# A two-layer transformer on one core: experts work on the rows routed to them, and routing runs ahead of attention

## What is computed

```python
xn = _layernorm(x)
x = x + attn0(xn) + ffn0(xn)     # 16 heads of 8; ffn0: silu gate, hidden 384, int weights / 127
xn = _layernorm(x)
x = x + attn1(xn) + moe(xn)      # attn1: block mask of 64 x 64; moe: 8 experts, hidden 256
```

```python
probs = softmax(xf @ gate_w.T)
top_p, top_i = top_k(probs, 2)
w = top_p / (sum(top_p) + 1e-9)
capacity = int(1.25 * T / E)                 # 320
oh = one_hot(top_i, E)
rank = cumsum(oh, axis=0) - 1                # over tokens, for each choice and expert
keep = sum(rank * oh, -1) < capacity
comb = einsum('tk,tke->te', w * keep, oh)
for e in range(E):
    y = silu(xf @ gate_proj_w[e].T) * (xf @ up_proj_w[e].T) @ down_proj_w[e].T
    out = out + comb[:, e:e + 1] * y
```

## Time and profile before

| | us |
|---|---|
| median of 3 runs | 647.14 (646.85 to 649.95) |
| the profiled execution | 649.82 |
| its span | 648.1 |

### The profile page before, as it was taken

The page is one execution under the profiler, slowest core; times in us unless marked ns, Lnnn a source line. Parts: engine busy times, 40 slices in busy tenths (PEclk is TensorE's granted clock), DMA queues, the critical chain, the costliest instruction groups (busy, mean ns, idle before and its releaser), DMA issues.

```text
span 648.1 us, 10352 instructions
## 1 busy us (share of the span) xinstructions
PE 563.7 (87%) x3834; PEld 226.0 (35%) x3834; DVE 509.8 (79%) x890; ACT 340.1 (52%) x402; POOL 121.5 (19%) x209
## 2 busy tenths in 40 slices
PE   4173789799889988989999999999999999999996
PEld 2020122142124223313454435353444343445443
DVE  4497679989986987897878888979888988774443
ACT  2000576666686665665535455545455545555562
POOL 6424061232314022221112020220001000000000
PEclk9655799999999998998999999999999999999999
DMA  2698726005302541445013331025050000000000
GB/s 69 159 185 126 237 86 123 2 30 122 49 1 98 56 45 13 110 44 53 2 51 70 33 39 18 2 99 51 3 67 0 3 1 0 19 2 17 1 1 17
DMA packets 125220, 34.08 MB, mean 53 GB/s; under 512 B 103458, under 2 KB 123442, under 8 KB 124338
## 3 DMA queue, kind: packets, MB, share of 16 engines
q1 hardware_dynamic: 125170, 33.41, 28.0%
HBM read 18.05 MB, written 13.63 MB: 49 GB/s over the span
## 4 chain that ended last, share of the span: by engine, by line
PE 59%; DVE 20%; SPq 7%; issue 5%; DMA 5%; ACT 4%; POOL 1%; ACTq 0%; DVEq 0%
PE ps L535 11%; PE ps L506 11%; DVE mx L797 10%; PE ps L545 9%; PE ps L536 8%; PE ps L490 7%; PE ps L475 4%; SPq L333 3%; DVE xs L852 3%; PE ps L438 2%; DMA QO<-mT 2%; DVE th L818 2%; SPq L321 2%; PE ps L559 2%; DVE h_T L831 2%
## 5 line engine op out<-in xcount | busy, mean ns | idle before, releaser
L683 ACT ACTIVATE PT<-ps 128x1024 f32<-128x1024 f32 x256 | 260.4, 1024 | 221.1 <-PE ps L490 219.6
L797 DVE TENSOR_REDUCE mx<-ps 128x2 f32<-128x1024 f32 x256 | 307.6, 1220 | 51.0 <-PE ps L475 49.7
L506 PE MATMUL ps<-PT,Vp 128*32 128x512 f32 x1024 | 138.1, 612 | 0.4 <-ACT o_sb L689 0.4
L475 PE MATMUL ps<-KO,QO 48*128 48x512 bf16 (+1 forms) x512 | 103.6, 406 | 33.2 <-DMA KO<-z 13.6
L490 PE MATMUL ps<-QO,KO 59*128 59x512 bf16 x512 | 101.1, 391 | 18.9 <-DMA QO<-mT 14.5
L818 DVE SCALAR_TENSOR_TENSOR th<-th,ps 128x512 f32<-128x512 f32 x76 | 52.1, 686 | 48.1 <-ACT th L698 47.0
L490 PEld LDWEIGHTS ps<-QO,KO 59*128 59x128 bf16 x512 | 24.7, 93 | 167.7 <-issue 85.3
L535 PE MATMUL ps<-xnT,eg 128*128 128x512 f32 x128 | 72.0, 644 | 10.6 <-DVE mx L797 10.2
L545 PEld LDWEIGHTS ps<-ed,h_T 128*128 128x128 f32 x512 | 62.1, 192 | 16.0 <-issue 14.8
L536 PE MATMUL ps<-xnT,eu 128*128 128x512 f32 x128 | 65.6, 594 | 0.0
L545 PE MATMUL ps<-ed,h_T 128*128 128x128 f32 x512 | 62.4, 275 | 0.3 <-DVE h_T L831 0.3
(11 more groups left out here) (134 smaller groups left out, 389.8 us busy)
## 6 DMA issues: line engine op xcount, KB each, us to landing
z<-part SPq DMA_DIRECT2D x16, 384.0 KB, 2.6
z<-part SPq DMA_DIRECT2D x16, 256.0 KB, 2.9
QO<-z SPq DMA_DIRECT2D x64, 48.0 KB, 2.7
KO<-z SPq DMA_DIRECT2D x64, 48.0 KB, 2.7
QO<-z SPq DMA_DIRECT2D x6, 384.0 KB, 7.3
KO<-z SPq DMA_DIRECT2D x6, 384.0 KB, 9.2
z<-part SPq DMA_DIRECT2D x16, 128.0 KB, 2.7
QO<-mT SPq DMA_DIRECT2D x96, 4.0 KB
```

What stands on the lines that cost most here:

```text
L475: mm = pe.matmul(ps[:, 2 * pair + half, :], rows_of(QO[u % 3], half, 2 * s + jj, rows, (qt, qt + 1)), rows_of(KO[u % 3], half, 2 * s + jj, ...
L506: last = pe.matmul(ps[32 * g:32 * g + 32, PV_BANK, :], Vp[u % 3][:, k, head(s, g), :], PT[:, (2 * t + g % 2) % 4, g // 2, :], start=(s % 2 ...
L683: act.activation(PT[:, e % 4], ps[:, 2 * pair:2 * pair + 2, :], ACT.Exp).then_inc(exp_done, 1)
L797: dve.tensor_reduce(mx[:, a, qt, col:col + 5:4], ps[:, 2 * pair:2 * pair + 2, :], AX_X, ALU.max, negate=True).then_inc(max_read, 1)
```

## The change

An expert now works on places: each has 640, of which 320 are for first and 320 for second choices. A token's two copies of its normalized row go to their places in a DRAM tensor by indirect DMA, with the row's destination and weight behind it; a copy that isn't kept goes to a row of its own behind the places. All experts run in the last two units: the list `expert_work` (transposing the places, gate pairs of 320 columns, outputs of 640 rows) is laid out two items a slot from slot 4 of unit 6 and three a slot in unit 7, which it leaves at slot 8. ScalarE scales the outputs by the weights, GpSimd sends them to the tokens by indirect DMA, and at the end two tensors of results are loaded and added. Routing and the transposed normalized input are made three units ahead in place of one and two, V one ahead in place of two. The buffers of V are two rather than three, those of the transposed input four.

```diff
-            if layer(u) == 1:
-                return SLOTS_U * seq(u) + slot
-            return HB * seq(u) + slot - 9 if 9 <= slot < 9 + HB else None
-        def expert_at(u, slot):
-            if u < B or u == B and slot < 2 or slot % 2:
-                return None
-            return E * seq(u) + slot // 2 - 1
+            return HB * u + slot - 9 if u < B and 9 <= slot < 9 + HB else None
+        expert_work = [("places", 0), ("places", 1)] + [("gate1", m) for m in range(4)]
+        for e in range(E):
+            expert_work += [("places", e + 2)] * (e + 2 < E)
+            if e + 1 < E:
+                first = 4 * (e + 1)
+                expert_work += [("gate1", first), ("gate1", first + 1), ("expert", e),
+                                ("gate1", first + 2), ("gate1", first + 3)]
+            else:
+                expert_work.append(("expert", e))
+        def expert_work_at(u, slot):
+            if u == U - 2 and slot >= EXPERTS_FROM:
+                a = 2 * (slot - EXPERTS_FROM)
+                return expert_work[a:a + 2]
+            if u == U - 1:
+                a = 2 * (SLOTS_U - EXPERTS_FROM) + 3 * slot
+                return expert_work[a:a + 3]
+            return []
...
+        def empty_places(sp):
+            sp.wait_ge(empty_ready, 2)
+            dst = x_places[0:N_PLACES].rearrange("(e p j) d -> p e j d", p=P, j=JE)
+            for e in range(E):
+                sp.dma_start(dst[:, e, :, 0:D], zero_f[:, 0:D].unsqueeze(1).to_broadcast([P, JE, D])).then_inc(emptied, 16)
+                sp.dma_start(dst[:, e, :, D:ROW], empty[:, e * JE:(e + 1) * JE, :]).then_inc(emptied, 16)
+            for k in range(2):
+                sp.dma_start(y_tokens[k * T:(k + 1) * T].rearrange("(p n) d -> p n d", p=P),
+                             zero_f[:, 0:D].unsqueeze(1).to_broadcast([P, T // P, D])).then_inc(emptied, 16)
...
+        def load_results(sp, b):
+            if b == 0:
+                sp.wait_ge(y_sent[0], 16 * JE * (E // 2))
+                sp.wait_ge(y_sent[1], 16 * JE * (E // 2))
+                sp.wait_ge(pv_done, SLOTS_U * (U - 1))
+            for k in range(2):
+                src = y_tokens[k * T + b * S:k * T + (b + 1) * S].rearrange("(t p) d -> p t d", p=P)
+                sp.dma_start(results_of(b)[:, k], src).then_inc(y_in[b], 16)
...
+        def scatter(pool, p):
+            b = seq(p)
+            if b == 0:
+                pool.wait_ge(emptied, N_EMPTIED)
+            pool.wait_ge(place_ready, b + 1)
+            pool.wait_ge(xn_twice, b + 1)
+            for t in range(NT):
+                for k in range(2):
+                    pool.indirect_dma_start(out=x_places[:], out_offset=bass.IndirectOffsetOnAxis(
+                        ap=place_i[:, b, t, k:k + 1], axis=0), in_=xe[p % 2][:, t, k, :],
+                        in_offset=None).then_inc(scattered, 16)
+        def send_results(pool, e):
+            if e == 0:
+                pool.wait_ge(meta_in, 16 * E)
+            pool.wait_ge(y_copied, e + 1)
+            for j in range(JE):
+                pool.indirect_dma_start(out=y_tokens[:], out_offset=bass.IndirectOffsetOnAxis(
+                    ap=meta[:].bitcast(I32)[:, e, j, 0:1], axis=0), in_=y_sb[e % 2][:, j, :],
+                    in_offset=None).then_inc(y_sent[e % 2], 16)
...
+        def places_copy(act, e):
+            act.wait_ge(places_ps, e + 1)
+            if e >= 2:
+                act.wait_ge(up_ps[1], 4 * (e - 1))
+            act.copy(places_T[e % 2][:], across(pair_of("places", e), 0, PLACES)).then_inc(places_ready, 1)
+        def result_copy(act, e):
+            act.wait_ge(expert_ps, e + 1)
...
+            if e >= 2:
+                act.wait_ge(y_sent[e % 2], 16 * JE * (e // 2))
+            for j in range(JE):
+                last = act.activation(y_sb[e % 2][:, j, :], across(pair_of("expert", e), j * P, (j + 1) * P),
+                                      ACT.Copy, scale=meta[:, e, j, 1:2])
+            last.then_inc(y_copied, 1)
...
+            if slot == 11 and f < U:
+                pe.wait_ge(on_ready, 2 * u + 1)
+                xnT_mms(pe, f, SIDE)
+            if slot == 12 and f < U and layer(f) == 1:
+                pe.wait_ge(xnT_ready, f + 1)
+                router_mms(pe, f)
...
         def last_vector(dve):
-            add_expert(dve, E * B - 1)
             normalize_out(dve, U - 1, 1)
+            for b in range(B - 1):
+                add_results(dve, b)
             residual(dve, U - 1)
+            add_results(dve, B - 1)
```

More of the change, by code:

```diff
@@ L256, in build @@
                 if gate_at(u, slot) is not None:
-                    taken.append((f"gate{layer(u)}", gate_at(u, slot)))
-                if expert_at(u, slot) is not None:
-                    taken.append(("expert", expert_at(u, slot)))
-        taken.append(("expert", E * B - 1))
+                    taken.append(("gate0", gate_at(u, slot)))
+                taken += expert_work_at(u, slot)
         turn = {job: i for i, job in enumerate(taken)}
@@ L337, in sync_unit @@
             p, n = u + 2, u + 1
+            if u == U - 2:
+                for e in range(2):
+                    load_places(sp, e)
+                load_meta(sp)
+                for e in range(2, 4):
+                    load_places(sp, e)
             max_rows(sp, u, 1)
@@ L422, in pool_unit @@
                 parts(pool, p, 1)
+            if f < U:
+                deviation(pool, f)
+                normalize(pool, f)
             if n < U:
                 residual_base(pool, n)
+            if f < U and layer(f) == 1:
+                second_rows(pool, f)
+            if u == U - 2:
+                send_results(pool, 0)
+            if n < U:
                 split_max(pool, n, 0)
+            if p < U and layer(p) == 1:
+                scatter(pool, p)
         def xnT_mms(pe, p, bank):
@@ new lines, in expert_out, with out_mms @@
+        def expert_out(pe, e):
+            pe.wait_ge(h_ready[1], 4 * (e + 1))
+            pair = take_pair(pe, "expert", e)
+            for j in range(JE):
+                for i in range(EB):
+                    last = pe.matmul(across(pair, j * P, (j + 1) * P), h1_T[:, e % 2, i, j * P:(j + 1) * P],
+                                     ed[:, e, i, :], start=(i == 0), stop=(i == EB - 1))
+            last.then_inc(expert_ps, 1)
+        def out_mms(pe, u, tiles):
+            L = layer(u)
+            if tiles[0] == 0:
+                pe.wait_ge(onT_ready, u + 1)
+                if L == 0:
+                    pe.wait_ge(h_ready[0], HB * (u + 1))
+            for t in tiles:
@@ L1113, in _ @@
                 sync_unit(sp, u)
-            store_x(sp, U - 1)
+            for b in range(B):
+                load_results(sp, b)
+            for b in range(B):
+                store(sp, b)
             sp.wait_ge(stored, 16 * B)
@@ L1131, in _ @@
                 pool_unit(pool, u)
+            for e in range(3, E):
+                send_results(pool, e)
         @block.vector
```

432 lines of the change are left out of this document (254 added, 178 removed).

## The result

The changed kernel took 608.09 us (median of 4 runs, 607.81 to 613.51) beside 648.55 us for the kernel before in the same comparison (646.85 to 650.00, 4 runs): a ratio of 0.939, interval [0.937, 0.942]. It is faster, but 33 us above the 575 predicted, and outside the range of 557 to 602.

A forecast was written before the change was run, and what follows sets the result against it. TensorE was taken to bound units 4 to 7, with neither TensorE nor VectorE full in units 1 to 3. 648.1 + 11.4 - 72.2 - 13.6 + 1.9 = 575.6 us of span; predicted 575 us, range 557 to 602.

The forecast's parts named there:

- the one on the indirect DMAs: GpSimd, units 2 to 5 and the result sends: 1.2 us per indirect DMA, 25 us free for eight scatters, all hidden.
- The clock: Rival: units 4 and 5 fall to half clock, 84 us each, 635 us in all; chance 0.02.
- Emptying transfers at 0: 18 SyncE transfers at the end of unit 0, 12 us of issue: 0 delay to maxima rows, bounds 0 and 15 us.
- units 4 and 5: They lose all expert work: 56.6 and 51.0 us, together 107.6 against 179.8, a change of -72.2.
- the tail: After unit 7: six additions, 4.1 us, fill 3.01 idle us and two more follow; 12.0 us, +1.9.
- unit 7's first half: Slots 0 to 7 of unit 7 take three expert items each: 53 us with 3 for the rest.
- the return path: Result sends from unit 7's slot 3.5, landed by 62 us, loads done at 71, where attention ends: hidden, nothing to spare.
- Unit 6: Slots 0 to 3 have nothing added, the other 12 two expert items each: 77 us, before 86.6.
- pairs and VectorE cost more: Rival: routing work and new waits add 5 us in each of four units, 595 us; range 588 to 605, chance 0.09.
- Slower than before: Rival: scatters over 3.1 us hold back maxima; gain is lost at 3.8 us each, 678 us at 4.3; chance 0.03.
- signs of being wrong: GpSimd gapless from unit 7's slot 4, ScalarE waiting there, units 4/5 clock below 0.95, unit 1 stopping at slot 8.

The follow-up runs named there:

- third comparison: The changed kernel run again unaltered, on another chip, beside the kernel before: 582.26 us, ratio 0.896, with no held-up start.
- the shorter rows: Changed kernel with each unit's eight token-row scatters in two groups of four, the second waiting for the next unit's maxima rows: 593.16 us, ratio 0.913.

## Why the prediction was wrong

Lengths in us; the columns "result" and "third" are the unaltered changed kernel with and without held-up starts:

| stage | forecast | result | third comparison |
|---|---|---|---|
| start | 67.0 | 67.0 | 67.0 |
| unit 0 | 58.5 | 55.8 | 56.2 |
| unit 1 | 59.2 | 61.3 | 61.9 |
| unit 2 | 60.6 | 65.5 | 62.0 |
| unit 3 | 62.7 | 68.1 | 66.8 |
| unit 4 | 56.6 | 65.6 | 56.9 |
| unit 5 | 51.0 | 56.2 | 51.8 |
| unit 6 | 77.0 | 75.0 | 73.4 |
| unit 7 | 71.0 | 79.6 | 72.3 |
| tail | 12.0 | 12.0 | 12.0 |
| span | 575.6 | 606.1 | 580.2 |

**The step that failed** is the one on the indirect DMAs, which put at nothing what they do to the other engines beyond a wait for GpSimd's queue. It asked how long GpSimd is held by each and whether the queue behind it has room. That was answered well (1.26 us a piece forecast as 1.2, room enough), and it was not the question. What the step left out is what a row of them does to the other engines. Against the third comparison the result lost 17.9 us in units 2 to 5 and 8.9 in units 6 and 7, 25.9 in all with the rest, of the 30.5 us by which its span was over the forecast. That the rows of indirect DMAs do it is shown: by the eight DMAs in the kernel before (+21.6 us against that kernel on the same chip), by the sends left out, after which the starts beside them are no longer held up, and by the shorter rows (593.16), the last without the unaltered kernel beside it. No row of before could have given the size, as it has no indirect DMA; but the prediction bounded only GpSimd's time by neighbours and gave no bound at all to the effect on others. My range was too narrow by this: without held-up starts the same program takes 582 us, inside it. Even that is in part luck, as the 4.6 us that its span is over the forecast are 10.5 us too many in units 1 to 5 and 7, less 2.3 in unit 0 and 3.6 in unit 6.

**The clock** was the second. The rival asked only if whole units fall to the half level, and priced that at 0.02. What happened is short spells after stalls of TensorE, 0.87 to 0.97 over a unit, and it was in the earlier trace rows: one stall of 2.10 us, and 0.95 in that stage. A change that empties TensorE makes more such places: the clock is 0.89 to 0.97 in units 1 to 5 of the third comparison, and 0.95 to 1.00 there before. Unit 3's 4.1 us over the forecast in the third comparison are of this kind: at 0.97 it took 62.6, with a forecast of 62.7.

**Emptying transfers at 0** was wrong within its bounds of 0 and 15: the wait for the maxima rows in unit 1 was 5.0 us, 3.1 more than with the transfers spread, and the unit is 3.6 us shorter so. The issues ran from 118.80 to 142.76 on SyncE, 24 us instead of 12, up to 2.46 for one expert's transfer where the earlier trace rows gave 0.65, and the last maxima rows were issued right behind them. The DMA engines were full as well over that time (share 1.20 in the stretch view, against 0.49 in unit 0 as a whole), so whether the rows came late by their issue or by the full engines isn't told apart; spreading eases both. The bound of 15 itself doesn't follow from the prediction's own numbers: 31 and 41 us less the 20 free are 11 and 21.

**Right**: units 4 and 5 at 56.9 and 51.8 where nothing is held up, for 56.6 and 51.0; the tail to a tenth; unit 7's first half at 52.8 for 53; the return path hidden, with little to spare: in the third comparison the result loads were issued by 63.9 us into unit 7 of 72.3 and landed 5.8 us after issue at the median. Unit 6 was 2.0 to 3.6 us better than forecast. The rival "pairs and VectorE cost more" holds in small: two routing products are locked out, 2.8 us in all. "Slower than before" did not come up, as GpSimd's price is 1.26 and not 3.8. Two of the signs of being wrong that it named did come: a clock under 0.95 in units 4 and 5 (0.87 and 0.94), and TensorE stopping 3.2 us in unit 1 for the maxima rows behind the emptying.

**Open**: what holds the starts up. The rows show that ScalarE and VectorE go on within 40 ns of each other (in unit 3, 2 us after the last DMA of the row has left GpSimd; an earlier hold ends in the middle of it), that GpSimd itself takes no longer, and that three of the five chips of the later comparisons do it, as did the first, and two don't. A signal that arrives late fits all this, but no view shows one, and no run tells it from a late end of the matmuls, whose ends are modelled. Nor does any tell GpSimd's making of these DMAs from their traffic: plain DMAs of GpSimd in such a row, or indirect ones of fewer rows, were not tried.

## What to carry to other kernels

Price a new kind of instruction twice: what it costs its own engine, and what it does to the others; where no row bears on the second, say so and widen the range, here by 26 us. Keep rows of GpSimd's indirect DMAs short, four rather than eight, where the chip may be one that holds starts up, but check that what is put off doesn't pile up elsewhere. And before an edit is credited, run the unaltered kernel beside it on the same chip: against the first result, leaving out the scatter "gained" 21 us that were the chip's.

## What the runs showed of the hardware

- The same program takes 582 us on one chip and 608 or 613 on others, while the kernel before takes 648.6 to 650.3 in all six comparisons. Most of the difference is starts of ScalarE and VectorE held up beside rows of GpSimd's indirect DMAs: at the longest by 3.2 to 6.3 us at a row of eight, 1.9 to 3.3 at the row of ten in unit 7, 6.0 at one of twelve, and 1.1 to 1.8 at rows of four or five.
- An indirect DMA of 128 rows shows as 0.96 us on GpSimd, 1.26 from start to start, 2.5 when its landing is waited for.
- A product of 64 columns on VectorE took 1.86 us instead of 0.21 beside an addition and a copy on GpSimd; one of 8x8 elements 1.20 instead of 0.22 beside the addition.
- The same 94 matmul records took 12.8, 15.4 and 18.7 us at mean granted clocks of 1.00, 0.84 and 0.68.
